# Second-layer row maxima of two neighbouring heads in one VectorE instruction, with one release for both PSUM banks

## The chip, the cores and the metric

The kernel runs on one core of a Trainium2 chip. The metric is the time of one execution on the device in microseconds (us), as the median of several runs; the kernel before has 1475.09 us (three runs, 1474.76 to 1475.23). TensorE is PE in the profile, VectorE is DVE, ScalarE is ACT, GpSimd is POOL and SyncE is SP.

## The reference, cut to what matters

Two transformer layers with a layer norm behind each half work on 2048 tokens of width 128, all in float32. Layer 0 is causal attention (8 heads, 2 key groups) and an FP4-quantised feed-forward part. Layer 1, where the change is, is full attention with 16 heads of width 8 in 4 key groups, and then a mixture of 8 experts:

```
q = (x @ Wq.T + bq).reshape(b, n, G, hpg, HD)
k = (x @ Wk.T + bk).reshape(b, n, G, HD)
v = (x @ Wv.T + bv).reshape(b, n, G, HD)
scores = jnp.einsum('bqghd,bkgd->bghqk', q, k) * scale
attn = jax.nn.softmax(scores, axis=-1)
y = jnp.einsum('bghqk,bkgd->bqghd', attn, v).reshape(b, n, d)
return y @ Wo.T + bo
```

The softmax needs the largest score of each query and head before any exponential is taken. The kernel gets it by computing the scores twice: once with queries on the partitions, only to take maxima, and once with keys on the partitions, with the maximum already subtracted, for the exponentials.

## The kernel before, in words

**Tiling.** The tokens are cut into 4 chunks of 512 queries (`NC`, `QC`), each chunk into 4 tiles of 128 (`QT`). One iteration of the attention works on one chunk and one key group: 4 heads (`HG`) and, in layer 1, 16 key tiles of 128. Layer 1 has 16 iterations (4 chunks by 4 groups), each of 64 units. A unit is one key tile and one head: a score matmul (`scores`, L718, written at L730), an exponential on ScalarE (L926) and a product with the values (`products`, L733, written at L749). Layer 0 has 8 iterations, with fewer key tiles in the early chunks.

**Maxima.** Beside the units of an iteration run the maxima of a later one. For layer 1 a maximum step is `("max", 1, h, q, kc, c, g, buf)`: TensorE makes the scores of 128 queries against 512 keys for head `h` in one PSUM bank (L650), and VectorE reduces the bank to one column of `MP` (L1161). There are 1024 such steps (16 iterations x 4 heads x 4 query tiles x 4 key chunks). `maxima` (L217) lists the heads in the order 1, 0, 3, 2. Heads 0 and 2 lie on the lower 64 partitions of the operands, heads 1 and 3 on the upper 64 (`band_of`, L214). When an iteration's maxima are done, `row_max` (L1242) reduces `MP` over the key chunks into `MS`, the `shift` step transposes it on TensorE, ScalarE copies it to `MR`, and SyncE sends it by four DMAs (L564) into one row of the query operand `Q1`, where the scores of that iteration read it.

**Banks.** PSUM has 8 banks. Banks 0 to 3 (`NS` = 4) serve all "side" steps, that is everything but units: maxima, projections, transposes, the parts of the feed-forward and the expert work. Side step `k` uses bank `k % 4`. In layer 1 three banks hold scores and one collects the products.

**Order.** All engines walk one list, `program`, which is made when the kernel is built (L504). Each engine executes its own instructions strictly in the order of that list, and waits on semaphores count steps. In an iteration of layer 1, `iteration` (L304) yields a score step, then about one side step per slot, and after every fourth score step the four products of an earlier key tile. Where chunk work of the layer (attention output, norm, gate, experts: `chunk1`, L257) is spread over an iteration too, there is more than one side step per slot.

**Release.** Each of the four side banks has a semaphore `side_free[bank]`; whoever reads the bank last raises it by one. TensorE waits before side step `k` for the release of step `k - 4` (L586). VectorE waits before step `k` for `side_full`, which TensorE raises once per side step (L1130). Steps that read another's result wait for that step's release (L780, L1300).

Of the kernel before, what the change touches and what calls it, by code (L numbers as in the profile page):

```python
# [68 lines left out]
def build(nc, A):  # L69
# [3 lines left out]
    with ctx:  # L73
# [432 lines left out]
            program += steps1(chunk, False, chunk == NC - 1)  # L506
        program = padded(program)

        def parts(engine, walk):

            walk(program, Count([]), 0)


        @block.sync
        def _(sp):
            sp.dma_start(const[:, :], A["consts"][:, 0:CONST_W]).then_inc(ld["const"], 16)
            sp.dma_start(qa[:, 0:P], A["consts"][:, CONST_W:]).then_inc(ld["masks"], 16)
            sp.dma_start(X[:, :, :], A["L0_attn_x"].rearrange("b (t p) d -> p (b t) d", p=P)).then_inc(ld["x"], 16)
            for dst, src in ((wq, A["L0_attn_wq"]), (wkd[:, :], A["L0_attn_wk_down"]),
                             (wvd[:, :], A["L0_attn_wv_down"]), (wup[:, 0, :], A["L0_attn_wk_up"]),  # L520
                             (wup[:, 1, :], A["L0_attn_wv_up"]),
                             (wo, A["L0_attn_wo"].rearrange("(h p) d -> p h d", p=P))):
                sp.dma_start(dst, src).then_inc(ld["attn0"], 16)
            for dst, src in ((wg, A["L0_ffn_w_gate"]), (wu, A["L0_ffn_w_up"])):
                sp.dma_start(dst[:, 0:2, :], src[0:2 * P, :].rearrange("(t p) d -> p t d", p=P)).then_inc(ld["ffn0"], 16)
                sp.dma_start(dst[0:FF - 2 * P, 2, :], src[2 * P:FF, :]).then_inc(ld["ffn0"], 16)
            sp.dma_start(wd[:, :], A["L0_ffn_w_down"]).then_inc(ld["ffn0"], 16)
            sp.dma_start(Wq1[:, :], A["L1_attn_Wq"]).then_inc(ld["attn1"], 16)
            sp.dma_start(Wo1[:, :], A["L1_attn_Wo"]).then_inc(ld["attn1"], 16)
# [12 lines left out]
            for dst, name, n in ((bv_b, "L1_attn_bv", LAT), (bo_b, "L1_attn_bo", D)):  # L542
                sp.dma_start(dst[:, :], A[name].rearrange("(a n) -> a n", a=1).broadcast_to([P, n])).then_inc(ld["attn1"], 16)
            sp.dma_start(gb_b[:, :], A["L1_ffn_gate_b"].rearrange("(a n) -> a n", a=1).broadcast_to([P, NE])).then_inc(ld["moe"], 16)
            sp.dma_start(gw[:, :], A["L1_ffn_gate_w"]).then_inc(ld["moe"], 16)
            sp.dma_start(ew[:, :, :], A["L1_ffn_expert_w"].rearrange("e k n -> k e n")).then_inc(ld["moe"], 16)
            sp.dma_start(eb[:, :], A["L1_ffn_expert_b"]).then_inc(ld["moe"], 16)

            out_v = A["out"].rearrange("b (t p) d -> p (b t) d", p=P)

            def walk(steps, n, lag):
                k, chunks = 0, 0
                for step in steps:
                    if step[0] == "shift":

                        sp.wait_ge(side_free[k % NS], n.side // NS + k // NS + 2)
                        if step[1] == 0:
                            dst = QO[SHIFT:KR, step[3], :, :].rearrange("o h (q p) -> o (h q) p", p=P)
                            sp.dma_start(dst.bitcast(f32), MR[:, :].bitcast(f32)).then_inc(shifted, 64)
                        else:  # L560
                            for h in range(HG):
                                row = band_of(h).start + PARTS1
                                dst = Q1[row:row + 1, step[3], h // 2, :].rearrange("o (q p) -> o q p", p=P)
                                sp.dma_start(dst.bitcast(f32), MR[h * QT:(h + 1) * QT, :].bitcast(f32)).then_inc(shifted, 16)  # L564
                    elif step[0] == "final":

                        chunks += 1
                        sp.wait_ge(tile_out, n.chunks + chunks)
                        c = step[1]
                        to = out_v[:, c * QT:(c + 1) * QT, :] if isinstance(c, int) else out_v[:, bass.ds(c * QT, QT), :]  # L570
                        sp.dma_start(to, OUT[:, :, :]).then_inc(stored, 16)
                    k += is_side(step)

            parts(sp, walk)
            sp.wait_ge(stored, 16 * (NC + 1))

# [4 lines left out]
        def _(pe):  # L581
            def side_item(item, n, k):

                kind = item[0]

                pe.wait_ge(side_free[k % NS], n.side // NS + k // NS + 1)  # L586
                bank = ps[:, k % NS, :]
                last = None
                if kind == "xT":
# [164 lines left out]
            def walk(steps, n, lag):  # L754
# [6 lines left out]
                for step in steps:  # L761
# [14 lines left out]
                    for name in needs(step):  # L776

                        if name in at:
                            j = at[name]
                            pe.wait_ge(side_free[j % NS], n.side // NS + j // NS + 2)  # L780
                            if kind == "max":
                                del at[name]
                    if kind == "scores":
# [39 lines left out]
        def _(act):  # L823
# [90 lines left out]
            def walk(steps, n, lag):  # L914
                k, u, logits = 0, 0, 0
                pv_at[0] = shifts_at[0] = heads_at[0] = 0
                for step in steps:
# [14 lines left out]
                    elif kind == "out_copy":  # L932

                        act.wait_ge(pv_done, n.units + NP_RING - lag + pv_at[0])

                        bank = OUT_BANKS[step[1] if len(step) > 2 else 0]
                        copy(OS[:, step[1] % 2, :], ps[:, bank, :]).then_inc(out_free, 1)
                    elif kind == "silu":

                        j = gate_at[0]  # L940
                        act.wait_ge(side_free[j % NS], n.side // NS + j // NS + 2)
                        nc.scalar.activation(H[:, :, :], H[:, :, :], ACT.Silu).then_inc(act_out, 1)
                    elif kind == "gate_exp":

                        act.wait_ge(logits_ready, n.logits + logits)
                        nc.scalar.activation(GP[:, :, :], GL[:, :, :], ACT.Exp).then_inc(act_out, 1)
                    elif is_side(step):
                        logits += kind == "logits"
                        if kind == "gate":
                            gate_at[0] = k  # L950
                        side_item(step, n, k, lag)
                        k += 1
# [10 lines left out]
        def _(pool):  # L963
# [44 lines left out]
            def walk(steps, n, lag):  # L1008
                k, rs, tiles, units = 0, 0, 0, 0
                for step in steps:  # L1010
# [9 lines left out]
                        last = k  # L1020
                    if kind == "sum":

                        pool.wait_ge(side_free[last % NS], n.side // NS + last // NS + 2)
                        sum_experts(step[1], 3 * (n.tiles + tiles))
                        tiles += 1
                    k += is_side(step)
# [7 lines left out]
        def _(dve):  # L1034
# [88 lines left out]
            def side_item(item, n, k, cnt):  # L1123
# [3 lines left out]
                bank, free = ps[:, k % NS, :], side_free[k % NS]  # L1127
                tiles = bank.rearrange("p (q d) -> p q d", d=D)

                dve.wait_ge(side_full, n.side + k + 1)  # L1130
                if kind in IN_PARTS:

                    dve.wait_ge(heads_copied, n.heads + cnt.heads)
# [18 lines left out]
                    i.then_inc(free, 1)  # L1152
                elif kind == "max":
                    _, layer, h, q, kc, c, g, buf = item
                    w = (q + 1) * P if layer == 0 and kc == c else QC
                    if layer == 0 and kc == c:

                        v.tensor_tensor_reduce(bank[:, 0:w], bank[:, 0:w], mask_qk[:, QC - w:QC], 1.0, LOWEST, ALU.add, ALU.max,  # L1158
                                               MP[:, buf, h, q, kc:kc + 1]).then_inc(free, 1)
                    else:  # L1160
                        v.tensor_reduce(MP[:, buf, h, q, kc:kc + 1], bank[:, 0:w], AX, ALU.max).then_inc(free, 1)  # L1161
                elif kind == "up":
                    q = item[1]
                    if q == 0:
# [107 lines left out]
            def walk(steps, n, lag):  # L1272
# [6 lines left out]
                for step in steps:  # L1279
# [17 lines left out]
                        continue  # L1297
                    if mine and own is not None and not (kind == "max" and own_kind == "max"):

                        dve.wait_ge(side_free[own % NS], n.side // NS + own // NS + 2)  # L1300
                        own = None
                    if kind in BANKLESS:
                        if kind == "final":
# [1 line left out]
                        bankless(step, n, cnt)  # L1305
                    if is_side(step):
                        side_item(step, n, k, cnt)
                        if kind not in ON_ACT:
                            own, own_kind = k, kind
                        k += 1  # L1310
                    if kind in ("y0", "y1", "down", "stats"):
                        cnt.rstd += 1
                if own is not None:
                    dve.wait_ge(side_free[own % NS], n.side // NS + own // NS + 2)


            dve.wait_ge(ld["const"], 16)
# [32 lines left out]
```

## Time and profile before

| | |
|---|---|
| median of 3 runs | 1475.09 us |
| the profiled execution: its time | 1470.66 us |
| its span, first to last instruction | 1468.9 us |
| busy share PE, PEld, DVE, ACT, POOL | 89%, 38%, 74%, 58%, 8% |
| mean granted TensorE clock | 0.929 of full |
| layer 1 attention, in the span | from about 605 us to about 1380 us |

PE is the matmuls and PEld the loads of stationary operands, which overlap the matmuls. A matmul's duration holds its latency; many overlap, so that the busy share of PE says how seldom it stood still, not how near it is to its peak. The chain of waits goes back from the last instruction, at each step to what released it; its shares say which engine held up the end.

### The profile page before, as it was taken

To read this page: it belongs to the slowest core of one execution; us is meant where nothing else is said; L and a number is where in the kernel's file an instruction comes from. 1 tells how busy PE (TensorE), PEld (TensorE's weight loads), DVE (VectorE), ACT (ScalarE), POOL (GpSimd) and SP (SyncE) were. 2 spreads that over 40 slices of the span, in tenths; PEclk is the share of its full clock that TensorE was granted. 3 is DMA by queue.
4 is the path that set the end of the run, shared out by engine and by line. 5 is a ranking of instruction groups with operands and counts; after the bars stand their busy time and mean duration, and the time that the engine had idled before them with its cause. 6 is when DMAs were issued, how large, how long until landed. Compare 5 with 4: busy or idle time off the path is not lost.

```text
span 1468.9 us, 19049 instructions
## 1 busy us (share of the span) xinstructions
PE 1311.4 (89%) x6337; PEld 563.3 (38%) x6337; DVE 1088.7 (74%) x2289; ACT 845.8 (58%) x1621; POOL 110.8 (8%) x227
## 2 busy tenths in 40 slices
PE   4688889889999965899999999999999999999884
PEld 3354445344443432433333333333433333333322
DVE  3677696688645668778888788888879888987324
ACT  2445535554555421177777666777666776777660
POOL 2010010001010100000000002000110000000033
PEclk9669899899999975689999999999999999999897
DMA  3000000000000000000000000000000000000000
GB/s 100 1 1 1 1 1 1 0 1 1 1 1 1 0 1 0 1 1 1 2 1 1 1 1 9 1 1 1 1 1 8 1 1 2 1 1 1 1 8 8
DMA packets 9010, 6.13 MB, mean 4 GB/s; under 512 B 2184, under 2 KB 8272, under 8 KB 8912
## 3 DMA queue, kind: packets, MB, share of 16 engines
q1 hardware_dynamic: 8912, 4.91, 1.2%
q8 instruction: 51, 0.84, 0.2%
q14 instruction: 47, 0.39, 0.1%
HBM read 3.66 MB, written 1.05 MB: 3 GB/s over the span
## 4 chain that ended last, share of the span: by engine, by line
PE 71%; DVE 15%; ACT 7%; issue 4%; POOL 1%; DMA 1%; SPq 1%; DVEq 0%; POOLq 0%; ACTq 0%
PE ps L749 24%; PE ps L730 16%; PE ps L650 8%; DVE MP L1161 7%; PE ps L726 6%; ACT PR L926 4%; PE ps L655 4%; PE ps L646 2%; PE ps L712 2%; ACT QO L825 1%; PE ps L661 1%; PE ps L679 1%; DVE ps L1158 1%; PE ps L615 1%; PE ps L690 1%
## 5 line engine op out<-in xcount | busy, mean ns | idle before, releaser
L926 ACT ACTIVATE PR<-ps 128x512 f32<-128x512 f32 (+2 forms) x1344 | 699.1, 585 | 414.1 <-PE ps L730 224.3
L1161 DVE TENSOR_REDUCE MP<-ps 128x1 f32<-128x512 f32 x1216 | 764.2, 682 | 133.9 <-PE ps L650 87.4
L749 PE MATMUL ps<-PR,V 128*32 128x512 f32 (+2 forms) x2688 | 435.6, 605 | 0.7 <-ACT OS L825 0.7
L730 PE MATMUL ps<-Q,KO 64*128 64x512 f32 x1024 | 363.1, 466 | 26.6 <-ACT PR L926 20.6
L650 PE MATMUL ps<-KO,Q 64*128 64x512 f32 x1024 | 354.5, 447 | 16.3 <-DVE MP L1161 12.2
L730 PEld LDWEIGHTS ps<-Q,KO 64*128 64x128 f32 x1024 | 153.6, 186 | 350.3 <-ACT PR L926 290.3
L650 PEld LDWEIGHTS ps<-KO,Q 64*128 64x128 f32 x1024 | 164.4, 191 | 85.0 <-DVE MP L1161 47.9
L726 PE MATMUL ps<-QO,KO 97*128 97x512 f32 (+3 forms) x320 | 144.7, 464 | 21.2 <-ACT PR L926 18.8
L655 PE MATMUL ps<-KO,QO 96*128 96x512 f32 (+2 forms) x320 | 127.9, 441 | 19.5 <-DVE QO L1137 13.7
L749 PEld LDWEIGHTS ps<-PR,V 128*32 128x32 f32 (+1 forms) x2688 | 74.1, 116 | 130.6 <-issue 60.4
L726 PEld LDWEIGHTS ps<-QO,KO 97*128 97x128 f32 x320 | 62.8, 201 | 152.0 <-ACT PR L926 97.0
L655 PEld LDWEIGHTS ps<-KO,QO 96*128 96x128 f32 x320 | 66.7, 214 | 43.2 <-DVE QO L1137 15.3
L1158 DVE CUSTOM_DVE_ANT_0 ps<-ps,mask_qk 128x128 f32<-128x128 f32 (+3 forms) x128 | 62.8, 493 | 20.8 <-PE ps L655 20.4
L996 POOL TENSOR_SCALAR_AFFINE_SELECT PR<-PR 128x128 f32<-128x128 f32 x128 | 39.0, 307 | 396.2 <-ACT PR L926 395.3
L988 POOL TENSOR_TENSOR RS<-VE,const 128x4 f32<-128x4 f32 x16 | 16.2, 1010 | 660.0 <-DVE VE L1091 660.0
L1102 DVE SCALAR_TENSOR_TENSOR Q<-ps,bq,Q 128x512 fp32r<-128x512 f32 x32 | 24.0, 750 | 39.9 <-ACT Q L840 30.2
L1137 DVE TENSOR_TENSOR QO<-ps,QO 32x512 fp32r<-32x512 f32 x32 | 22.0, 688 | 25.7 <-ACT QO L825 25.4
L1003 POOL TENSOR_TENSOR qa<-qa 128x512 f32<-128x512 f32 (+2 forms) x24 | 19.7, 821 | 225.3 <-DVE XQ L1206 216.2
L712 PE MATMUL ps<-ew,XQT 128*128 128x512 f32 x64 | 36.2, 665 | 0.0
L646 PE MATMUL ps<-XT,WQ 128*128 128x512 f32 x64 | 35.6, 638 | 0.0
L825 ACT ACTIVATE HQT<-ps 128x256 f32<-128x256 f32 (+2 forms) x36 | 11.0, 354 | 37.4 <-PE ps L685 33.8
L840 ACT ACTIVATE Q<-ps,bq_low,const 128x512 fp32r<-128x512 f32 x32 | 24.9, 777 | 7.7 <-PE ps L646 7.7
(179 smaller groups left out, 748.7 us busy)
## 6 DMA issues: line engine op xcount, KB each, us to landing
Q<-MR SPq DMA_DIRECT2D x64, 2.0 KB
result<-V SPq DMA_DIRECT2D x4, 256.0 KB, 2.3
H<-in_L_attn_wq SPq DMA_DIRECT2D x1, 512.0 KB, 6.7
HQT<-in_L_attn_wo SPq DMA_DIRECT2D x1, 512.0 KB, 5.0
ew<-in_L_ffn_expert_w SPq DMA_DIRECT2D x1, 512.0 KB
bq<-in_L_attn_bq SPq DMA_DIRECT2D x12, 0.1 KB
wd<-in_L_ffn_w_down SPq DMA_DIRECT2D x1, 176.0 KB, 3.7
wg<-in_L_ffn_w_gate SPq DMA_DIRECT2D x1, 128.0 KB, 4.4
```

The source lines that it names most:

```text
L646: last = nc.tensor.matmul(bank[:, :], WQ13[:, g, pair, :, :], XT[:, c * QC:(c + 1) * QC], start=True, stop=True)
L650: last = nc.tensor.matmul(bank[:, :], Q1[rows, buf, h // 2, q * P:(q + 1) * P], KO1[rows, g, kc * QC:(kc + 1) * QC], start=True, stop=True)
L655: last = nc.tensor.matmul(bank[:, 0:n], QO[0:SHIFT, buf, h, q * P:(q + 1) * P], KO0[0:SHIFT, g, kc * QC:kc * QC + n], start=True, stop=True)
L712: last = nc.tensor.matmul(bank[:, :], X2T[:, q * P:(q + 1) * P], ew[:, 4 * e:4 * e + 4, :], start=True, stop=True)
L726: m = nc.tensor.matmul(dst[:, q0:QC], KO0[:, g, kt * P:(kt + 1) * P], QO[:, buffer_of(0, it), h, q0:QC], start=True, stop=True)
L730: m = nc.tensor.matmul(dst[:, :], KO1[rows, g, kt * P:(kt + 1) * P], Q1[rows, it, h // 2, :], start=True, stop=True)
L749: nc.tensor.matmul(dst, VO[layer][:, kt, g, :], PR[:, u % NP_RING, q0:QC], start=kt == 0, stop=kt == key_tiles(layer, c) - 1).then_inc(pv_ ...
L825: return nc.scalar.activation(out, in_, ACT.Copy)
L926: nc.scalar.activation(PR[:, u % NP_RING, q0:QC], ps[:, 8 - nb + u % nb, q0:QC], ACT.Exp, scale=SCALE[layer]).then_inc(exp_done, 1)
L996: nc.gpsimd.affine_select(block, block, [[1, P]], ALU.is_ge, nothing, base=0, channel_multiplier=-1).then_inc(clipped, 1)
L1158: v.tensor_tensor_reduce(bank[:, 0:w], bank[:, 0:w], mask_qk[:, QC - w:QC], 1.0, LOWEST, ALU.add, ALU.max, MP[:, buf, h, q, kc:kc + 1]).th ...
L1161: v.tensor_reduce(MP[:, buf, h, q, kc:kc + 1], bank[:, 0:w], AX, ALU.max).then_inc(free, 1)
```

## The change

Once the list is made, the change walks the side steps and marks step `k` as paired with `k + 1` when both are layer-1 maxima of heads `h` (odd) and `h - 1` with all else equal, and `k` is not in bank 3, so that the two banks are neighbours. A table `released` then gives, for each side step, the semaphore and the value that tell that its bank is free: both steps of a pair share one entry, on the first bank's semaphore. Every wait that computed this by arithmetic takes it from the table (`freed`).

- VectorE issues nothing for the first of a pair and does not wait there. At the second it waits for `side_full` of the second and runs one `tensor_reduce` over both banks, 128 partitions x 2 x 512, into two columns of `MP`, and raises the first bank's semaphore once.
- TensorE's instructions and their order are untouched; before a side step it waits for the entry of step `k - 4`, which for a pair is the end of the common reduce.
- Bank order is head `h`, then `h - 1`, while the output columns rise, so the two heads change places in `MP`. Unpaired layer-1 maxima write to column `h ^ 1` too, and the four DMAs read the rows of `MR` at `h ^ 1`.

```
+        sides = [step for step in program if is_side(step)]
+        def is_pair(k):
+            a, b = sides[k], sides[k + 1] if k + 1 < len(sides) else ("",)
+            return (k % NS < NS - 1 and a[:2] == b[:2] == ("max", 1) and a[2] % 2 == 1 and b[2] == a[2] - 1
+                    and a[3:] == b[3:])
+        paired = [is_pair(k) for k in range(len(sides))]
+        released, releases = [], [1] * NS
+        for k in range(len(sides)):
+            if k and paired[k - 1]:
+                released.append(released[-1])
+            else:
+                releases[k % NS] += 1
+                released.append((side_free[k % NS], releases[k % NS]))
+        def freed(k):
+            return released[k] if k >= 0 else (side_free[k % NS], 1)
...
-                pe.wait_ge(side_free[k % NS], n.side // NS + k // NS + 1)
+                pe.wait_ge(*freed(k - NS))
...
-                dve.wait_ge(side_full, n.side + k + 1)
+                if not paired[k]:
+                    dve.wait_ge(side_full, n.side + k + 1)
...
                     _, layer, h, q, kc, c, g, buf = item
+                    if paired[k]:
+                        return
+                    if k and paired[k - 1]:
+                        b = (k - 1) % NS
+                        v.tensor_reduce(MP[:, buf, h:h + 2, q, kc], ps[:, b:b + 2, :], AX, ALU.max).then_inc(side_free[b], 1)
+                        return
+                    i = h ^ layer
...
-                        v.tensor_reduce(MP[:, buf, h, q, kc:kc + 1], bank[:, 0:w], AX, ALU.max).then_inc(free, 1)
+                        v.tensor_reduce(MP[:, buf, i, q, kc:kc + 1], bank[:, 0:w], AX, ALU.max).then_inc(free, 1)
```

## Rows read from the trace of the kernel before

**Rows 1.** The page: busy time of each engine, and the chain by line.

```profile
PE 1311.4 (89%) x6337; PEld 563.3 (38%) x6337; DVE 1088.7 (74%) x2289; ACT 845.8 (58%) x1621; POOL 110.8 (8%) x227
PE ps L749 24%; PE ps L730 16%; PE ps L650 8%; DVE MP L1161 7%; PE ps L726 6%; ACT PR L926 4%; PE ps L655 4%; PE ps L646 2%; PE ps L712 2%; ACT QO L825 1%; PE ps L661 1%; PE ps L679 1%; DVE ps L1158 1%; PE ps L615 1%; PE ps L690 1%
```

**Rows 2.** The chain by line in layer 1 alone, 605 to 1377 us.

```profile
by line: PE ps L749 28.5%; PE ps L730 28.4%; PE ps L650 13.0%; DVE MP L1161 7.6%; ACT PR L926 6.5%; PE ps L646 3.6%; PE ps L712 2.2%; issue 2.0%; PE ps L661 0.9%; DVE Q L1102 0.7%; POOL qc L1003 0.6%; DVE ST L1086 0.6%; SPq L564 0.5%; PE ps
```

**Rows 3.** The chain by line in one iteration without chunk work, 928 to 975 us.

```profile
by line: PE ps L730 34.8%; PE ps L749 34.5%; PE ps L650 13.2%; ACT PR L926 10.3%; PE ps L646 4.5%; issue 2.1%; PE ps L661 1.3%; PE ps L658 0.4%; ACT OS L825 0.0%; ACTq L925 0.0%
```

**Rows 4.** The same in an iteration with expert work, 871 to 928 us.

```profile
by line: DVE MP L1161 26.6%; PE ps L749 17.7%; PE ps L730 16.1%; PE ps L712 11.1%; PE ps L650 8.8%; POOL qc L1003 4.4%; ACT PR L926 2.1%; PE ps L646 1.9%; issue 1.8%; DVE V L1097 1.6%; DVE ST L1086 1.5%; DVE qc L1212 1.2%; DVE Q L1102 1.2%;
```

**Rows 5.** Busy time by stretch (us and instructions of each engine, then clock, DMA).

```profile
871.00:928.00 57.00, 55.50 (x280) 20.36 (x280) 48.55 (x90) 36.25 (x70) 9.78 (x13) 1.00 0.02 6
928.00:975.00 47.00, 45.32 (x266) 17.74 (x265) 41.20 (x70) 35.30 (x69) 0.00 (x0) 1.00 0.01 1
```

**Rows 6.** Groups by line and shape: busy us, mean ns; idle before, releasers.

```profile
L1161 DVE TENSOR_REDUCE MP<-ps 128x1 f32<-128x512 f32 x1216 | 764.2, 682 | 133.9 <-PE ps L650 87.4 <-PE ps L655 41.0
L1158 DVE CUSTOM_DVE_ANT_0 ps<-ps,mask_qk 128x512 f32<-128x512 f32 x32 | 22.1, 691 | 3.8 <-PE ps L655 3.7
L1158 DVE CUSTOM_DVE_ANT_0 ps<-ps,mask_qk 128x128 f32<-128x128 f32 x32 | 9.4, 293 | 2.7 <-PE ps L655 2.6
```

**Rows 7.** Waits between 627 and 1377 us: us in total, times, longest.

```profile
DVE MP L1161 <- PE ps L650: 57.8, 101, 2.8
PEld ps L650 <- DVE MP L1161: 27.5, 77, 1.6
```

**Rows 8.** Timeline of four units without chunk work: start us, us, engine, line, [idle before].

```profile
956.46 0.50 PE L730 MATMUL ps<-Q,KO 64*128 64x512 f32 x2
956.80 0.40 PE L650 MATMUL ps<-KO,Q 64*128 64x512 f32 x2
957.03 0.39 PE L730 MATMUL ps<-Q,KO 64*128 64x512 f32 x1
957.22 1.89 DVE L1161 TENSOR_REDUCE MP<-ps 128x1 f32<-128x512 f32 x3 [0.34 <-PE ps L650]
957.26 0.39 PE L650 MATMUL ps<-KO,Q 64*128 64x512 f32 x1
957.64 0.49 PE L730 MATMUL ps<-Q,KO 64*128 64x512 f32 x1
957.97 0.49 PE L650 MATMUL ps<-KO,Q 64*128 64x512 f32 x2
958.39 1.06 PE L749 MATMUL ps<-PR,V 128*32 128x512 f32 x8
959.39 0.50 PE L730 MATMUL ps<-Q,KO 64*128 64x512 f32 x1
```

**Rows 9.** Timeline where VectorE never rests, from 900.56 us.

```profile
900.56 16.23 DVE L1161 TENSOR_REDUCE MP<-ps 128x1 f32<-128x512 f32 x27
901.31 0.18 PEld L650 LDWEIGHTS ps<-KO,Q 64*128 64x128 f32 x1 [0.43 <-DVE MP L1161]
903.53 1.06 PE L749 MATMUL ps<-PR,V 128*32 128x512 f32 x8
906.51 1.07 PE L749 MATMUL ps<-PR,V 128*32 128x512 f32 x8
```

**Rows 10.** Timeline at the start of layer 1, at the lower clock.

```profile
611.48 9.66 DVE L1161 TENSOR_REDUCE MP<-ps 128x1 f32<-128x512 f32 x16
622.04 0.79 PE L650 MATMUL ps<-KO,Q 64*128 64x512 f32 x1 [0.21 <-DVE MP L1161]
625.75 1.22 PE L650 MATMUL ps<-KO,Q 64*128 64x512 f32 x2
```

**Rows 11.** Busy time at the start of layer 1 (605 to 627 us).

```profile
605.00:627.00 22.00, 18.58 (x41) 8.62 (x40) 16.02 (x30) 3.53 (x5) 0.00 (x0) 0.58 0.00 0
```

More of the change, by code:

```diff
@@ L554, in walk @@
                     if step[0] == "shift":
-                        sp.wait_ge(side_free[k % NS], n.side // NS + k // NS + 2)
+                        sp.wait_ge(*freed(k))
                         if step[1] == 0:
@@ L563, in walk @@
                                 dst = Q1[row:row + 1, step[3], h // 2, :].rearrange("o (q p) -> o q p", p=P)
-                                sp.dma_start(dst.bitcast(f32), MR[h * QT:(h + 1) * QT, :].bitcast(f32)).then_inc(shifted, 16)
+                                sp.dma_start(dst.bitcast(f32), MR[(h ^ 1) * QT:((h ^ 1) + 1) * QT, :].bitcast(f32)).then_inc(shifted, 16)
                     elif step[0] == "final":
@@ L779, in walk @@
                             j = at[name]
-                            pe.wait_ge(side_free[j % NS], n.side // NS + j // NS + 2)
+                            pe.wait_ge(*freed(j))
                             if kind == "max":
@@ L940, in walk @@
                         j = gate_at[0]
-                        act.wait_ge(side_free[j % NS], n.side // NS + j // NS + 2)
+                        act.wait_ge(*freed(j))
                         nc.scalar.activation(H[:, :, :], H[:, :, :], ACT.Silu).then_inc(act_out, 1)
@@ L1021, in walk @@
                     if kind == "sum":
-                        pool.wait_ge(side_free[last % NS], n.side // NS + last // NS + 2)
+                        pool.wait_ge(*freed(last))
                         sum_experts(step[1], 3 * (n.tiles + tiles))
@@ L1158, in side_item @@
                         v.tensor_tensor_reduce(bank[:, 0:w], bank[:, 0:w], mask_qk[:, QC - w:QC], 1.0, LOWEST, ALU.add, ALU.max,
-                                               MP[:, buf, h, q, kc:kc + 1]).then_inc(free, 1)
+                                               MP[:, buf, i, q, kc:kc + 1]).then_inc(free, 1)
                     else:
-                        v.tensor_reduce(MP[:, buf, h, q, kc:kc + 1], bank[:, 0:w], AX, ALU.max).then_inc(free, 1)
+                        v.tensor_reduce(MP[:, buf, i, q, kc:kc + 1], bank[:, 0:w], AX, ALU.max).then_inc(free, 1)
                 elif kind == "up":
@@ L1298, in walk @@
                     if mine and own is not None and not (kind == "max" and own_kind == "max"):
-                        dve.wait_ge(side_free[own % NS], n.side // NS + own // NS + 2)
+                        dve.wait_ge(*freed(own))
                         own = None
@@ L1307, in walk @@
                         side_item(step, n, k, cnt)
-                        if kind not in ON_ACT:
+                        if kind not in ON_ACT and not paired[k]:
                             own, own_kind = k, kind
@@ L1313, in walk @@
                 if own is not None:
-                    dve.wait_ge(side_free[own % NS], n.side // NS + own // NS + 2)
+                    dve.wait_ge(*freed(own))
             dve.wait_ge(ld["const"], 16)
```

## The prediction

> **What bounds the kernel now.** I read the page first. TensorE is busy for 89% of the span, VectorE for 74%, and the chain that ends last runs mostly over TensorE: the products, the scores and the maxima's matmuls, while the reduce L1161 that the change touches has 7% of it [rows 1]. All the change lies in layer 1, so I asked for the chain there alone: L1161 has 7.6% of the 772 us from 605 to 1377, that is 59 us [rows 2]. Then I split it by kind of iteration. In one without chunk work, the reader is to see that L1161 is not in the chain at all: TensorE's own lines and the wait for exponentials (ACT PR, 10.3%) fill it [rows 3]. In one with expert work L1161 leads with 26.6%, or 15 us of 57 [rows 4]. So VectorE holds the end up only in parts of the iterations with chunk work and in a short stretch at the start of layer 1. It is well loaded everywhere, though: 41.2 of 47 us in a plain iteration, 48.6 of 57 in a loaded one [rows 5]. So TensorE is the bound and VectorE a near second that must hand banks back in time. A change to VectorE can win only the little that is in the chain, and it can lose wherever it hands a bank back later.
>
> **How many pairs, from the list of steps in the code.** The list has 1616 side steps, 1024 of them layer-1 maxima. By the diff's rule 341 pairs form: 117 on banks 0 and 1, 107 on banks 1 and 2, 117 on banks 2 and 3. So 682 maxima go in pairs and 342 stay single; where a pair begins in bank 3 it isn't made. TensorE, ScalarE and the DMAs do what they did; the exchange of two rows in the DMAs' addresses costs nothing, as their number and sizes stay.
>
> **What a pair costs on VectorE.** A single reduce lasts 682 ns [rows 6], but back to back 27 of them take 16.23 us, so 601 ns each [rows 9]: about 80 ns overlap with the next. One operation of VectorE on PSUM stands in the trace at two sizes, 293 ns for 128 columns and 691 ns for 512 [rows 6]: 398 ns for 384 columns, or 1.037 ns a column. A second bank adds 512 x 1.037 = 531 ns. I take 682 + 531 = 1213 ns for the pair, and 601 + 531 = 1132 ns for its pace back to back, against 1202 for two singles: 70 ns saved per pair. The trace has no read across two banks. The lower end is that nothing but the columns counts, 1062 ns for the pair; the upper end is no gain, two full durations, 1364 ns. I take 1213, as the slope comes from the nearest rows; the ends move each late release below by 0.15 us either way.
>
> **What the saved time is worth.** Only where L1161 is in the chain: 59 us / 0.601 = 98 reduces, two thirds of them paired, so 33 pairs x 70 ns = 2.3 us. Were the whole 149 ns (2 x 682 - 1213) won each time, it would be 5 us.
>
> The Trainium skill, "Perfetto Trace Analysis", section "Optimizing Scalar/DVE Operations", gives about 125 ns as the per-instruction overhead of VectorE on PSUM and says that grouping operations helps if the engine is saturated; by that figure the 33 pairs would save an estimated 4 us. The same section says that where the engine isn't saturated but causes bubbles on others, breaking instructions up may let work complete sooner, which speaks against this change. Rows 3 and 5 put most of layer 1 in that second case.
>
> **What the common release costs.** Four units without chunk work look like this [rows 8]. The first scores start at 956.46, the first maxima's matmul at 956.80, and VectorE, idle till then, starts at 957.22: 0.42 to 0.44 us from the matmul's start. The next maxima's matmuls come at about 957.26 and 957.97, the products at 958.39 and the next scores at 959.39, so a period is 2.93 us, of which the products take 1.0. From the end of a reduce to TensorE's load the trace shows 0.07 us (900.56 + 0.68 = 901.24, load at 901.31) [rows 9].
>
> Now take a pair a, b and the step a + 4 that reuses a's bank. It may start 0.44 + 1.21 + 0.07 = 1.72 us after b's matmul started. Before, it had to wait only for a's own reduce, 0.44 + 0.68 + 0.07 = 1.19 us after a's start, and a is earlier than b by a slot. Whether 1.72 us hurts depends on what TensorE does between b and a + 4. If a set of products lies between, that alone is 1.0 us and the distance is over 2 us: no wait. If none does, b is the first maximum behind the products and a + 4 the last before the next ones: from 956.80 to 957.97, 1.17 us. TensorE then stands 1.72 - 1.17 = 0.55 us, and the products, the next scores and all else queue behind it. Nothing gives it back: the wait for the exponential within the group (the scores at 957.64) lies before the stall and is in the 1.17 us already.
>
> From the list of steps I counted, for each pair, what stands between b and a + 4. In layer 1's iterations 89 of the pairs have no products between; half of them (46) are exactly score, max, score, max, score, the others have two maxima side by side, a shift or an expert step. 64 of these 89 lie in iterations or parts without chunk work, 25 in those with it. In the first, 64 x 0.55 = 35 us. In the second, TensorE waits for L1161 already (27.5 us of load waits in all of layer 1, most of them there [rows 7]) and VectorE is behind; I take half the price, 25 x 0.27 = 7 us. The bounds of a stall: nothing, if the distance is longer than I read it, and 0.9 us, where two maxima side by side shorten the distance by a slot and the reduce has the upper price. By iteration the count is four to nine in most, so one of 47 us would grow by 2 to 5 us.
>
> At the start of layer 1 the clock is 0.58 [rows 11], which is near the lower level of 1.2 GHz. 16 reduces take 9.66 us with nothing but maxima on TensorE [rows 10]. With pairs, TensorE refills two banks after each release: 0.07 + 0.79 for the first matmul, 0.43 more for the second (1.22 - 0.79), 0.05 to the start, 1.34 us; with 1.21 of reduce that is 2.55 us for four maxima against 2.40 now. That loses some 1 us over the stretch, where one would have looked for a gain. Fifteen more pairs without products between lie in the last part of layer 0 or here; beyond this 1 us I count them at nothing, since TensorE waits there for other things (bounds -1 to +5).
>
> **Sum.** +35 + 7 + 1 - 2.3 = +41 us. The profiled execution has 1470.66 us with a span of 1468.9; it comes to 1511. The median before is 4.4 us above that execution, so 1515 on the scale of the medians. My readings of start times are to some hundredths and the 0.55 rests on one group's spacing; with a stall of 0.50 in the plain parts the sum is +38. I say 1512.
>
> **Rivals.**
> (a) Faster: VectorE is what matters and slack covers the later release. For it: 7.6% of the chain in layer 1 and 88% load. Place: the stretches like that of rows 9; price: -2.3 to -5 us, and if TensorE is freed also from other waits on L1161, up to 341 x 70 ns = -24 us. It decides if a + 4 comes 1.72 us or more after b nearly always. That gives 1470 (1451 at the least). Against it: rows 3, in which L1161 isn't in the chain.
> (b) Half absorbed: the late release is real, but waits that TensorE has for exponentials (10.3% of 47 us, 4.8 us an iteration [rows 3]) move under it. In the eleven plain iterations up to 2 us each come back, and part of the 7 us in the others; the sum is +10 to +20, so 1485 to 1495. For it: two waits of the same group could overlap. Against it: the order, by which the exponential's wait comes first in the group.
> (c) The stalls feed on each other: reading across banks costs the full 1364 ns and two-max gaps count 0.85 us. Then 64 x 0.75 + 25 x 0.4 = +58 us, 1533.
> (d) Nothing changes, within 0.2%: gain and stalls are both small. 1475.
> That the reduce is issued as two by the hardware or the change does not take hold is not likely: the pairing is fixed in the list.
>
> **Numbers.** Forecast 0.65; (b) 0.12; (c) 0.05; (d) 0.05; (a) 0.13. The likeliest case alone has 1492 to 1530. A measurement can tell about 0.2% (3 us) from no change. Faster 0.13, same 0.05, slower 0.82. For 8 in 10 the range leaves out most of (a) and the top of (c): 1474 to 1530.
>
> **What would show it.** Right: the paired reduce near 1.21 us, 341 of them; load waits L650 <- L1161 grown from 27.5 us to some 60 or more with the products waiting behind; a plain iteration of 49 to 51 us instead of 47; DVE busy falling by about 341 x 149 ns = 51 us of durations while the span grows. Wrong: a plain iteration of 47 us still, with loaded ones shorter (rival a); or iterations longer while waits for ScalarE shrink as much (rival b). It also fails if a pair is far from 1.2 us.

## The result and the profile after

The kernel with the change takes 1532.86 us (median of four runs, 1520.96 to 1541.57), against 1475.16 us before (four runs, 1474.76 to 1475.24): 1.0386 times as long, 95% interval 1.0315 to 1.0457. The forecast was slower, 1512 us with a range to 1530. The direction was right, the size was not: +58 us instead of +37, and outside the range. The profiled execution has 1534.24 us with a span of 1532.5, 63.6 us above that of before.

The two forms of the reduce after the change, from the page (columns as in rows 6): L1182 is the reduce over two banks, L1191 the single one. The first answers to L1161 in rows 6.

```profile
L1182 DVE TENSOR_REDUCE MP<-ps 128x2 f32<-128x1024 f32 x341 | 407.4, 1220 | 115.1 <-PE ps L672 113.7
L1191 DVE TENSOR_REDUCE MP<-ps 128x1 f32<-128x512 f32 x534 | 353.8, 684 | 88.9 <-PE ps L672 43.8
```

The chain by line in the kernel after, first over the 15 iterations of layer 1 from 632.7 to 1440.1 us, then in a plain iteration, one without chunk work (959 to 1010 us).

```profile
by line: PE ps L771 27.3%; PE ps L752 22.0%; DVE MP L1182 15.8%; PE ps L672 14.4%; ACT PR L948 3.9%; PE ps L668 3.5%; issue 2.2%; DVE MP L1191 2.0%; PE ps L734 1.7%; PE ps L683 1.0%; DVE Q L1124 0.9%; DVE ST L1108 0.4%; ACT Q L862 0.4%; POO
...
by line: PE ps L771 31.2%; PE ps L752 24.3%; PE ps L672 17.0%; DVE MP L1182 17.0%; PE ps L668 4.2%; ACT PR L948 3.5%; issue 1.5%; PE ps L683 1.2%; PE ps L680 0.4%
```

The maxima's reduce had 7.6% of the chain in layer 1 [rows 2] and no part in a plain iteration [rows 3]; now it has 17.8% and 17.0%. The waits of layer 1 in the kernel after (632 to 1440 us), which answer to rows 7:

```profile
DVE MP L1182 <- PE ps L672: 99.1, 117, 2.6
PEld ps L672 <- DVE MP L1182: 76.4, 113, 1.3
PE ps L672 <- DVE MP L1182: 39.6, 86, 0.9
PEld ps L672 <- DVE MP L1191: 9.9, 17, 1.6
```

TensorE's load waits on the reduces grew from 27.5 us to 76.4 + 9.9. VectorE waits more too (57.8 us before, 99.1 now for the common reduces alone): both engines stand in turn. One place in a plain iteration of the kernel after, with a set of products before it and one behind (timeline, columns as in rows 8):

```profile
985.56 0.50 PE L752 MATMUL ps<-Q,KO 64*128 64x512 f32 x2
985.90 0.40 PE L672 MATMUL ps<-KO,Q 64*128 64x512 f32 x2
986.14 0.39 PE L752 MATMUL ps<-Q,KO 64*128 64x512 f32 x1
986.34 5.87 DVE L1182 TENSOR_REDUCE MP<-ps 128x2 f32<-128x1024 f32 x5 [1.12 <-PE ps L672]
986.38 0.39 PE L672 MATMUL ps<-KO,Q 64*128 64x512 f32 x1
986.75 0.50 PE L752 MATMUL ps<-Q,KO 64*128 64x512 f32 x1
987.62 0.19 PEld L672 LDWEIGHTS ps<-KO,Q 64*128 64x128 f32 x2 [0.69 <-DVE MP L1182]
987.62 0.50 PE L672 MATMUL ps<-KO,Q 64*128 64x512 f32 x2 [0.37 <-DVE MP L1182]
988.05 1.06 PE L771 MATMUL ps<-PR,V 128*32 128x512 f32 x8
```

The second maximum of the pair starts at 985.90, the common reduce at 986.34 (0.44 later), and the step that reuses the first bank is let go at 987.62: 1.72 us after the second maximum, to the hundredth what the prediction worked out for a reduce of 1.21 us (a place picked because it is the tight form; the average price is below). Before, that step came 1.17 us after it (956.80 to 957.97 [rows 8]). The products behind it are late by the difference.

**Where the 63.6 us lie.** I call a pair tight when no products stand between its second maximum and the reuse of its first bank. An iteration's length is the distance between the first products of every sixteenth set. These lengths repeat to 0.1 us between executions where the clock is the same, so they show what the whole time, which varies by several us, can't:

```
iteration            1    2    3    4    5    6    7    8    9   10   11   12   13   14   15
kind                 p    p    p    p    L    L    p    p    L    L    p    p    L    p    p
before, us        47.0 46.1 46.6 47.5 58.6 56.2 47.1 47.5 57.6 56.2 47.0 47.1 52.6 46.0 49.0
after, us         52.3 51.2 49.7 49.6 62.2 61.1 51.2 51.6 60.6 62.5 48.9 48.9 58.3 49.8 49.5
tight pairs          6    8    6    3    5    9    7    7    6    9    4    4    9    7    0
(p plain, L loaded with chunk work)
```

The granted clock of the iterations differs between the two executions in four places: iteration 1 has 0.98 before and 0.94 after, 6 has 1.00 and 0.97, 10 has 1.00 and 0.95, 15 has 0.94 and 0.91. In the others it is the same, 1.00 or 0.97.

Iterations with few tight pairs grew little, the one with none by 0.5 us. In sum the ten plain ones grew by 31.8 us with 52 tight pairs and the five loaded ones by 23.5 us with 38, 0.61 and 0.62 us for each. In the eight plain iterations that have the full clock both before and after it is 26.1 us for 46 pairs, 0.57 us each, and in the three loaded ones whose clock is the same (5, 9, 13) 12.3 us for 20, 0.62 each. The rest is 2.8 us ahead of them and 5.4 us behind them. No paired step lies in that last stretch; it is a matter of the clock there (below).

### The profile page after: what moved, and what is told of

The parts are those of the page before. It is cut to its first block, busy times and chain, and to the rows that moved or that the text cites. A ratio compares the mean times of both kernels' runs of the same rounds, so it can differ in the third digit from the quotient of the medians.

```text
span 1532.5 us, 18708 instructions
## 1 busy us (share of the span) xinstructions
PE 1336.8 (87%) x6337; PEld 568.6 (37%) x6337; DVE 1073.9 (70%) x1948; ACT 848.4 (55%) x1621; POOL 111.3 (7%) x227
## 4 chain that ended last, share of the span: by engine, by line
PE 68%; DVE 21%; ACT 5%; issue 3%; POOL 1%; DMA 1%; SPq 1%; DVEq 0%; POOLq 0%; ACTq 0%
PE ps L771 23%; PE ps L752 13%; DVE MP L1182 9%; PE ps L672 9%; PE ps L748 6%; DVE MP L1191 4%; PE ps L677 4%; ACT PR L948 3%; PE ps L668 2%; PE ps L734 2%; ACT QO L847 1%; PE ps L683 1%; PE ps L701 1%; PE ps L637 1%; DVE ps L1188 1%
## 5 line engine op out<-in xcount | busy, mean ns | idle before, releaser
L1182 DVE TENSOR_REDUCE MP<-ps 128x2 f32<-128x1024 f32 x341 | 407.4, 1220 | 115.1 <-PE ps L672 113.7
L771 PE MATMUL ps<-PR,V 128*32 128x512 f32 (+2 forms) x2688 | 440.3, 613 | 0.7 <-ACT OS L847 0.7
L1191 DVE TENSOR_REDUCE MP<-ps 128x1 f32<-128x512 f32 x534 | 353.8, 684 | 88.9 <-PE ps L672 43.8
L752 PE MATMUL ps<-Q,KO 64*128 64x512 f32 x1024 | 367.8, 472 | 20.3 <-ACT PR L948 14.2
L672 PEld LDWEIGHTS ps<-KO,Q 64*128 64x128 f32 x1024 | 158.1, 192 | 150.2 <-DVE MP L1182 89.8
L1160 DVE TENSOR_TENSOR QO<-ps,QO 32x512 fp32r<-32x512 f32 x32 | 22.0, 688 | 25.6 <-ACT QO L847 25.3
```

The lines of the kernel that those rows point to most:

```text
L672: last = nc.tensor.matmul(bank[:, :], Q1[rows, buf, h // 2, q * P:(q + 1) * P], KO1[rows, g, kc * QC:(kc + 1) * QC], start=True, stop=True)
L752: m = nc.tensor.matmul(dst[:, :], KO1[rows, g, kt * P:(kt + 1) * P], Q1[rows, it, h // 2, :], start=True, stop=True)
L771: nc.tensor.matmul(dst, VO[layer][:, kt, g, :], PR[:, u % NP_RING, q0:QC], start=kt == 0, stop=kt == key_tiles(layer, c) - 1).then_inc(pv_ ...
L1182: v.tensor_reduce(MP[:, buf, h:h + 2, q, kc], ps[:, b:b + 2, :], AX, ALU.max).then_inc(side_free[b], 1)
L1191: v.tensor_reduce(MP[:, buf, i, q, kc:kc + 1], bank[:, 0:w], AX, ALU.max).then_inc(free, 1)
```

## The experiments

All start from the kernel with the change. "Layer 1" is the growth of the 15 iterations over 752.0 us before, with plain and loaded in brackets.

**Pairs that products cover, alone.** The place of products in the list decides whether a pair is made.

```
+        place = [i for i, step in enumerate(program) if is_side(step)]
+        def products_between(k):
+            if k + 4 >= len(sides):
+                return True
+            return any(step[0] == "products" for step in program[place[k + 1]:place[k + 4]])
-        paired = [is_pair(k) for k in range(len(sides))]
+        paired = [is_pair(k) and products_between(k) for k in range(len(sides))]
```

> Pairs are made only where a set of products stands on TensorE between the pair's second maximum and the step that reuses its first bank: 237 of the 341 pairs stay, the 104 without products between are single reduces again. Theory (the late release hurts only where nothing covers it): no stall is left and VectorE saves up to 237 x 70 ns of work, of which little is in the chain; 1470 to 1478 us, a plain iteration of 47 us. Rival (the common release or the wide read costs something at every pair): the loss of 58 us stays in proportion, 237/341 x 58 = +40 us, 1515. Second rival (clock): the loss comes from lower granted clock after stalls; as the stalls go it goes too, which this run can't tell from the theory.

Measured: 1475.46 us, 1.0006 times before (0.9984 to 1.0028). Layer 1 +2.4 us (+2.0, +0.4). The 237 common reduces are there and last as long as in the change:

```profile
L1200 DVE TENSOR_REDUCE MP<-ps 128x1 f32<-128x512 f32 x742 | 486.0, 684 | 112.3 <-PE ps L681 65.7 <-PE ps L686 42.5
L1191 DVE TENSOR_REDUCE MP<-ps 128x2 f32<-128x1024 f32 x237 | 284.5, 1218 | 34.4 <-PE ps L681 33.2
```

So two thirds of the pairs cost nothing that can be told. VectorE's busy time is 11 us shorter than before (1077.7 against 1088.7 us), and what that saves is hardly visible: the loaded iterations 6 and 10 are 0.5 us shorter each at the same clock, while iterations 1 and 9, which lengthened by 1.2 us each, have a clock lower by 0.02 and 0.03 here. A cost at every pair is out.

**The tight pairs, alone** (the condition turned round, `not products_between(k)`).

> Only the 104 pairs without products between are made, 89 of them in layer 1; the other 237 are single. Theory: nearly the whole loss stays, 1520 to 1535 us, and a plain iteration has 49 to 52 us as with all pairs. Rival (cost at every pair): 104/341 x 58 = +18 us, 1493.

Measured: 1527.99 us, 1.0347 times before (1.0280 to 1.0413). Layer 1 +52.2 us (+29.6, +22.6). 104 common reduces alone bring nearly all of the loss:

```profile
L1191 DVE TENSOR_REDUCE MP<-ps 128x2 f32<-128x1024 f32 x104 | 127.3, 1224 | 77.2 <-PE ps L681 76.3
```

**Common release, single reduces.**

```
-                if not paired[k]:
-                    dve.wait_ge(side_full, n.side + k + 1)
+                dve.wait_ge(side_full, n.side + k + 1)
...
                     if paired[k]:
+                        v.tensor_reduce(MP[:, buf, h ^ 1, q, kc:kc + 1], bank, AX, ALU.max)
                         return
                     if k and paired[k - 1]:
-                        b = (k - 1) % NS
-                        v.tensor_reduce(MP[:, buf, h:h + 2, q, kc], ps[:, b:b + 2, :], AX, ALU.max).then_inc(side_free[b], 1)
+                        v.tensor_reduce(MP[:, buf, h ^ 1, q, kc:kc + 1], bank, AX, ALU.max).then_inc(side_free[(k - 1) % NS], 1)
                         return
```

> The same 341 pairs share one release, but VectorE runs a single reduce for each bank as soon as that bank is full; only the release is common. Theory (a + 4 may go 0.44 + 0.68 + 0.07 = 1.19 us after b's matmul started, and TensorE gets there after 1.17 us in the tight places): next to no stall, +0 to +8 us, 1475 to 1483. Rival (that a bank comes back with its neighbour is by itself the cost): near the change, 1515 to 1535.

Measured: 1500.84 us, 1.0174 times before (1.0119 to 1.0229). Layer 1 +25.3 us (+8.4, +16.9). Both theories missed. In the plain iterations the result is close to the reckoning, in the loaded ones it is not. The reckoning lets VectorE be idle when the second maximum is full. Where it isn't, the common release waits for its queue as well. That is my reading and not the whole of it: three of the loaded iterations (9, 10, 13) have a lower clock here than before (0.97, 0.92, 0.91 against 1.00, 1.00, 0.97), some 20 us more at the lower level, which may account for up to 10 of the 16.9 us (an estimate: half the speed for that time). Iterations 5 and 6, whose clock is as before, grew by 4.4 us with 14 tight pairs, 0.32 us each.

**Late start, single reduces, common release** (as above, but the first waits for `side_full` of the second).

> The same pairs; VectorE waits until both banks are full, runs two single reduces and releases both at the end. Theory: 0.44 + 0.60 + 0.68 + 0.07 = 1.79 us from b's start instead of 1.72, and 70 ns more VectorE time per pair: a little worse than the change, 1535 to 1550 us. Rival (the read across two banks is what hurts): well below the change, 1475 to 1500.

Measured: 1530.09 us, 1.0373 times before (1.0318 to 1.0428); layer 1 +55.7 us (+33.0, +22.7). That is the change's loss without any read across two banks, so the read itself is not what hurts. That it should be a little worse than the change shows only in the plain iterations (+33.0 against +31.8); in the total the two can't be told apart, and it lies 5 us under the expected range. This execution also settles whether the loss needs a lower clock: its iterations 6 and 10 run at the full clock, as before, and still have 60.4 and 60.8 us against 56.2 and 56.2.

```profile
893.60:954.00 60.40, 54.53 (x276) 19.41 (x275) 48.82 (x88) 36.22 (x69) 9.79 (x13) 1.00 0.02 6
1118.90:1179.70 60.80, 54.76 (x275) 19.40 (x274) 48.64 (x88) 36.43 (x69) 9.82 (x13) 1.00 0.02 5
```

None of the five loaded iterations has a lower clock here than before, and they grew by 22.7 us, 0.60 for each tight pair.

**Late start, each bank released by its own reduce** (the late wait, single reduces, and `released` filled per step as if nothing were paired).

> VectorE waits until both banks of a pair are full, then runs two single reduces, and each bank is released by its own reduce. Theory for the plain iterations (a is free 0.44 + 0.68 + 0.07 = 1.19 us after b's matmul started, TensorE arrives after 1.17): hardly a stall, +0 to +5 us there. In the loaded ones the first bank comes back one reduce earlier than under joint release, so less than that run's +17 us: +3 to +12. Total 1478 to 1490. Rival (the late start is what costs, not the release at the end of both): near the change, 1520 or more.

Measured: 1492.86 us, 1.0126 times before (1.0092 to 1.0159); layer 1 +23.3 us (+13.2, +10.1). The total lies above what was expected, because of the plain iterations. One place in them (timeline of this kernel):

```profile
964.38 2.48 DVE L1181 TENSOR_REDUCE MP<-ps 128x1 f32<-128x512 f32 x4 [0.46 <-PE ps L669]
964.79 0.49 PE L749 MATMUL ps<-Q,KO 64*128 64x512 f32 x1
965.12 0.18 PEld L669 LDWEIGHTS ps<-KO,Q 64*128 64x128 f32 x1
965.12 1.09 PE L669 MATMUL ps<-KO,Q 64*128 64x512 f32 x2
965.72 0.18 PEld L669 LDWEIGHTS ps<-KO,Q 64*128 64x128 f32 x1 [0.41 <-DVE MP L1181]
```

The first reuse (965.12) goes without a wait, as reckoned; but here a fifth maximum stands before the products, and it waits for the pair's second reduce. A group of four units has four or five maxima, and I had reckoned with four, though rows 8 show five too (matmuls x2 at 956.80, x1 at 957.26, x2 at 957.97).

**Common reduce over half of each bank.**

```
-                        v.tensor_reduce(MP[:, buf, h:h + 2, q, kc], ps[:, b:b + 2, :], AX, ALU.max).then_inc(side_free[b], 1)
+                        v.tensor_reduce(MP[:, buf, h:h + 2, q, kc], ps[:, b:b + 2, 0:QC // 2], AX, ALU.max).then_inc(side_free[b], 1)
```

> All 341 pairs as in the change, but the common reduce reads only the first 256 columns of each bank, so that the maxima of paired steps are taken over half the keys; nothing else is left out. The reduce should last about 1.22 - 0.53 = 0.69 us. Theory (a stall is the reduce's length plus 0.51 us less the 1.17 us that TensorE needs): the release comes 1.19 us after b's matmul, the stalls go, and VectorE is much less loaded: 1470 to 1480. Rival (fewer, joint releases cost by themselves, whatever the length): 1500 or more.

Measured: 1469.44 us, 0.9970 times before (0.9943 to 0.9996); layer 1 -0.3 us (+4.2, -4.6). With the shorter reduce the loss is gone, though 341 common releases are left.

**Common reduce over three quarters of each bank** (`0:3 * QC // 4`).

> All 341 pairs, the common reduce reads the first 384 columns of each bank, so the maxima of paired steps are taken over three quarters of the keys; nothing else is left out. The reduce should last about 0.95 us, the release comes 1.46 us after b's matmul. Theory (a stall is that less 1.17 us, 0.3 us, in 90 places): +20 to +30 us with the part due to VectorE's backlog, 1495 to 1503. Rival (a threshold: any wait drops the clock or a whole slot is lost): as the change, 1520 or more, or none, 1475.

Measured: 1497.85 us, 1.0171 times before (1.0142 to 1.0200); layer 1 +23.1 us (+15.9, +7.2). The common reduces of the two kernels, half first, with the order of the columns as before:

```profile
L1182 DVE TENSOR_REDUCE MP<-ps 128x2 f32<-128x512 f32 x341 | 230.4, 689 | 191.3 <-PE ps L672 189.8
```

```profile
L1182 DVE TENSOR_REDUCE MP<-ps 128x2 f32<-128x768 f32 x341 | 319.2, 955 | 151.1 <-PE ps L672 150.5
```

With 689, 955 and 1220 ns the layer grows by -0.3, 23.1 and 55.4 us, with number, place and release of the pairs unchanged. From 955 to 1220 ns that is 32 us for 0.265 us more in 90 tight pairs, 0.36 us a pair. In the eight plain iterations with the full clock in both it is 11.6 us for 46 pairs, 0.25, the bare difference; the surplus lies in the loaded iterations (16.3 us for 38 pairs, 0.43) and in iteration 1 (3.9 us for 6). Part of it is the clock, which in the change is lower in iterations 1, 6, 10 and 13 than here. But iterations 5 and 9, at equal clock, have 0.35 us a pair too; I put that down to pairs that find VectorE busy, which no run shows by itself.

The half read also says something of the worth of VectorE's time. VectorE is busy for 899.4 us in it against 1088.7 before, 189 us less, and the layer is no shorter; only the loaded iterations win 4.6 us. It isn't a clean test: its first banks still come back late (0.44 + 0.69 + 0.07 = 1.20 us after the second maximum), which its +4.2 us in the plain iterations may be. Less work with single reduces and own releases was not run.

**Pairs only in plain, or only in loaded iterations** (`is_pair(k) and not loaded(k)`, where `loaded` tells whether the running iteration is one of the five; then the complement).

> Pairs only outside the five iterations of layer 1 that carry chunk work: 237 pairs, 66 of them without products between (51 in layer 1). Theory (each such pair costs about 0.6 us wherever it lies): about 51 x 0.61 = +31 us in layer 1, the plain iterations as long as with all pairs, the loaded ones as before; 1503 to 1512 us. Rival (the loss in the loaded iterations is carried over from stalls elsewhere, or the two kinds influence each other): loaded iterations longer than 56 to 58 us although they have no pair.

> The complement: 104 pairs in the five loaded iterations, 38 without products between. Theory (full price there too): 38 x 0.61 = +23 us, 1495 to 1502. The prediction on record counted 25 stalls there at half price: +7 us, 1482. Rival (VectorE is the bound there, so pairs help): 1472 or less.

Measured: plain only 1504.59 us, 1.0210 times before (1.0174 to 1.0247), layer 1 +33.0 us (+31.4, +1.6). Loaded only 1499.96 us, 1.0184 times before (1.0140 to 1.0227), layer 1 +28.7 us (+0.2, +28.5). Each kind grows where its pairs are and hardly elsewhere. The loaded iterations, which the prediction had at +7, bear 23 to 28 us by themselves. Why 28.5 here and 23.5 in the change: the surplus lies in iterations 6, 10 and 13 (2.7, 1.1 and 1.2 us), and 6 and 10 have a lower clock here (0.89 and 0.92) than in the change (0.97 and 0.95). Windows of 4 us of the loaded-only kernel, in its iteration 6 (TensorE, its loads, VectorE, ScalarE, GpSimd, then the granted clock):

```profile
902.00:906.00 4.00, 3.23 (x16) 1.00 (x14) 3.97 (x7) 2.16 (x5) 0.00 (x0) 1.00 0.23 66
906.00:910.00 4.00, 3.74 (x15) 1.50 (x15) 1.89 (x3) 1.77 (x4) 0.00 (x0) 0.64 0.01 2
910.00:914.00 4.00, 3.54 (x14) 0.97 (x15) 3.02 (x3) 1.29 (x3) 0.00 (x0) 0.50 0.00 0
914.00:918.00 4.00, 3.74 (x18) 1.67 (x18) 3.01 (x3) 2.08 (x4) 0.00 (x0) 0.50 0.00 0
918.00:922.00 4.00, 3.60 (x21) 1.44 (x17) 2.33 (x3) 2.07 (x4) 0.00 (x0) 0.65 0.00 0
922.00:926.00 4.00, 3.54 (x24) 1.21 (x19) 2.87 (x3) 2.07 (x4) 0.00 (x0) 1.00 0.00 0
```

Right after the expert work, behind a stretch in which TensorE was busy for 3.23 us of 4, the clock falls to its lower level of 1.2 GHz for some 14 us, and that iteration has 63.8 us against 61.1 in the change, whose fall there is shorter. Before, the same iteration had the full clock throughout.

**Products put behind a pair that they would split,** with pairs and with single reduces.

```
+        def products_behind_pairs():
...
+                if j - i == 4 and program[i][1] == 1:
+                    b = j if j in at else j + 1
+                    if (b in at and paired[at[b] - 1] and place[at[b] - 1] < i
+                            and all(step[0] in ("scores", "max") for step in program[j:b + 1])):
+                        out[i:b + 1] = program[j:b + 1] + program[i:j]
...
+        program = products_behind_pairs()
```

> All 341 pairs as in the change, but the list of steps is reordered: where a set of four products would stand between the two maxima of a pair, it is put behind the second (67 sets, each later by one or two steps). A tight pair then gets the products between its second maximum and the reuse of its first bank; 30 of the 90 pairs without products between remain in layer 1. Theory (0.61 us for each such pair, nothing for the others): 30 x 0.61 = +18 us, 1490 to 1496. Rival (the loss goes with the number of pairs, or with stalls that find another place): 1515 or more.

> The same reordered list with single reduces and own releases, as the base of the run before it. Theory: the order alone costs or gives little, 1470 to 1480. If it is slower than that, its excess has to be taken off the other run.

Measured: with pairs 1489.34 us, 1.0122 times before (1.0091 to 1.0153), layer 1 +15.4 us (+10.2, +5.2); single 1477.66 us, 1.0037 times before (1.0013 to 1.0061), layer 1 +4.8 us. All 341 common reduces are still there, and about 10.6 of 55.4 us of loss are left over the single form of the same order. That is 0.35 us for each of the 30 tight pairs that remain, less than the 0.61 expected, and the total lies 0.7 us under the expected range; which of them are cheap stays open. It isn't a better kernel than the one before: the new order itself costs a little (+4.8 us in the profiled execution, two of whose iterations, 6 and 9, have a slightly lower clock than before).

**Only the exchange of the two heads** (`paired` all false).

> No pairs; only the exchange of two heads in MP and in the four DMAs' rows stays. Theory: no change, 1471 to 1479, every iteration of layer 1 as before within 0.3 us.

Measured: 1472.28 us, 1.0002 times before (0.9988 to 1.0017); no iteration differs by more than 0.1 us. The exchange of columns and rows is free.

## Why the prediction was wrong in size, and where it was right

**Right.** The bound (TensorE, with VectorE giving banks back just in time), the common reduce (1213 ns forecast, 1220 measured), the exchange at no cost, and the step that matters: a late release that hurts only in tight pairs. The covered pairs alone give no change, the tight ones alone nearly all of it, and the length of the reduce sets the price. At one place it is 1.72 us from start to reuse, as worked out, and the price of a stall, 0.55 us, is met where the clock is full both before and after: 0.57. The reduces' durations fell by 48 us in sum (1216 x 682 ns = 829.3 before, 341 x 1220 + 534 x 684 = 781.3 after), as forecast; VectorE's busy time, in which overlapping durations count once, fell by only 14.8 us (1088.7 to 1073.9).

**The rivals.** A win for VectorE (a) is refuted by the result, and by the covered pairs, which save work and lose nothing and still gain nothing that the total shows. Half absorption by the waits for exponentials (b) is refuted too, but its sign did show: in a plain iteration ScalarE's share of the chain fell from 10.3% [rows 3] to 3.5%, 4.8 us to 1.8, so some of those waits do lie under the new stalls. They gave nothing back, for a tight pair costs no less than its own stall. Rival (c) named 1533 us, which is the time measured; that is luck, as its mechanism did not occur: a read across the banks takes 1220 ns and not 1364.

**The sum by its terms.** The prediction had +35 for the plain iterations, +7 for the loaded, +1 for the start and -2.3 for saved VectorE time.

- Plain, +35: measured +31.8. The prediction took 64 stalls at 0.55; there are 52 tight pairs at 0.61. Steps of loaded iterations that lie outside the stretch of chunk work had been counted as plain, 12 of them, so that like for like the prediction had 52 x 0.55 = 29 us for the plain iterations.
- Loaded, +7: measured +23.5. This is the step that failed. "In the second, TensorE waits for L1161 already (27.5 us of load waits in all of layer 1, most of them there [rows 7]) and VectorE is behind; I take half the price, 25 x 0.27 = 7 us." There are 38 tight pairs in these five iterations, and each costs as much as elsewhere, 0.62 us. Like for like, with the 12 counted as plain, the prediction had 7 + 12 x 0.55 = 14 us there, 10 us too little. Stalls that were there before don't pay for the new ones. That a common release comes later from whatever point VectorE begins, and later still where it is behind, is the likely reason and is argued only. The clock isn't the reason: the three loaded iterations with the same clock before and after have 0.62 too, and in the late start with single reduces the five have 0.60 at no lower clock.
- Saved time, -2.3: nothing that can be told. The covered pairs alone take 11 us off VectorE's busy time, and the layer is 2.4 us longer, with a slightly lower clock in two iterations; two loaded iterations are 0.5 us shorter each.
- Start, +1: measured +2.8 ahead of the first iteration; other kernels have values from -2.7 to +6.8 there, with and without pairs, so that this isn't told apart from the clock.
- Not foreseen: +5.4 us in the last stretch, where no pair lies. The same stretch before, and then after:

```profile
1381.90:1468.90 87.00, 61.72 (x284) 24.16 (x283) 26.41 (x86) 33.92 (x65) 26.21 (x35) 0.85 0.02 7
```

```profile
1440.10:1532.50 92.40, 67.04 (x284) 25.85 (x283) 26.41 (x86) 33.98 (x65) 26.23 (x35) 0.78 0.02 6
```

The instructions are the same in number, VectorE's time is the same, and TensorE's matmuls take 5.3 us longer at a clock of 0.78 instead of 0.85. The half-read kernel, which is no slower than before, has 92.4 us and 0.78 there too, while the late start with single reduces, which has the whole loss, has 86.6 us and 0.85, and the covered-pairs kernel 87.0 and 0.85. So this part doesn't go with the stalls. Whether the pairs make it likelier is open: the kernel before and the two others with plain single reduces have 0.85 or more there, but so have four with pairs, and each kernel has one profile.

These terms account for the difference between the sum's +41 and the +63.6 us of the two profiled executions: 7 us for the half price (25 x 0.28), 6 for a stall of 0.62 on average in place of 0.55 (where the clock fell, and in the loaded iterations), 0.6 for one tight pair more than counted (90, not 89), 2.3 for the saved time, 1.8 for the start, 5.3 for the last stretch. With the full price the sum would have been 1515 + 7 = 1522 us, still inside the range; the failed step is the largest single error of mechanism, but it alone would not have put the time outside the range. The forecast of 1512 was also 3 us under its own sum, and the reason given for that, a stall of 0.50, gives 1513. The range's upper end was set by doubtful prices of a stall in the plain part; no width was given for the half price, the guess with the least behind it, nor for the clock, which differs from one execution to the next.

## What to carry to other kernels

- A merged instruction gives its buffers back at its end. Ask for each merge how long the producer takes from the second operand to the reuse of the first buffer; if that is shorter than the merged instruction with its two hand-overs (here 1.17 against 1.72 us), each such place costs the difference, however much work the merge saves.
- An engine's share of the chain is not what less work on it wins: here 59 us of layer 1's chain fell on these reduces, and with 189 us less busy time on VectorE (the half read) the layer won 0.3 us, the loaded iterations 4.6. The chain says where the end was held up, not that nothing else stood right behind.
- Don't take a discount for new waits in a stretch that waits already, unless a row shows that the two overlap.

## What the runs showed of the hardware that was not expected

- The time of one and the same kernel goes with its mean clock. The four executions of the kernel after have 1520.96, 1531.48, 1534.24 and 1541.57 us at mean clocks of 0.932, 0.921, 0.919 and 0.914, in that order. That width is no mark of the stalls alone: before had four times within 0.5 us in the first measurement, but 1469.39 us at 0.931 to 1483.12 at 0.917 in the later ones, and the half read 1462.99 at 0.935 to 1477.91 at 0.919. In the profiled execution of the kernel after the lower level appears behind the expert work, in iteration 10, where the one before has the full clock throughout; the other three executions have no profile:

```profile
1146.00:1150.00 4.00, 3.37 (x17) 1.11 (x16) 3.96 (x7) 1.73 (x4) 0.00 (x0) 1.00 0.23 66
1150.00:1154.00 4.00, 3.60 (x17) 1.50 (x15) 2.04 (x3) 1.91 (x4) 0.00 (x0) 0.68 0.00 0
1154.00:1158.00 4.00, 3.54 (x14) 0.92 (x15) 3.07 (x3) 1.34 (x3) 0.00 (x0) 0.50 0.00 0
```

- VectorE reads two neighbouring PSUM banks in one instruction at the pace of one: 689, 955 and 1220 ns for 512, 768 and 1024 columns in all, 1.04 ns a column, and 684 ns for a single bank of 512. Half of each of two banks takes 689 ns, so the border between them costs some 5 ns.
